# Three unread products ahead of each step's sum in the two gather passes of a graph network kernel

## Time and profile before

| | |
|---|---|
| median of three runs | 7530.44 us |
| the profiled execution: its own time | 7527.34 us |
| its span | 7525.2 us |
| TensorE (PE) busy | 6260.3 us, 83% of the span |
| TensorE weight loads (PEld) busy | 4862.5 us, 65% |
| VectorE (DVE) busy | 3390.7 us, 45% |
| ScalarE (ACT) busy | 1942.3 us, 26% |
| GpSimd (POOL) busy | 2203.3 us, 29% |
| mean granted clock of TensorE | 0.888 |

### The profile page before, as it was taken

How to read it: one execution, slowest core, us unless ns; L and a number is a source line. 1 busy time by engine, 2 the same in 40 slices (tenths; PEclk the granted TensorE clock), 3 DMA queues, 4 the chain that set the end, 5 groups by cost and what they waited for, 6 DMA issues and landing times.

```text
span 7525.2 us, 106468 instructions
## 1 busy us (share of the span) xinstructions
PE 6260.3 (83%) x27439; PEld 4862.5 (65%) x27440; DVE 3390.7 (45%) x9448; ACT 1942.3 (26%) x5163; POOL 2203.3 (29%) x2534
## 2 busy tenths in 40 slices
PE   5888899999999999677776676999999966767766
PEld 3443577778887787555555554777778755555555
DVE  8876666631111222555565564222233324444443
ACT  3899600000000111111111112232233322222222
POOL 2000100010001111566666631000111126666664
PEclk8987899999999999777778788999999978888787
DMA  4777877797788777433333328888877743333332
GB/s 156 255 257 271 294 265 264 262 330 275 275 303 313 253 260 253 123 83 83 85 83 83 83 59 302 303 291 322 320 242 250 242 153 101 100 100 100 99 100 74
DMA packets 599449, 1517.98 MB, mean 202 GB/s; under 512 B 72695, under 2 KB 241506, under 8 KB 599203
## 3 DMA queue, kind: packets, MB, share of 16 engines
q1 hardware_dynamic: 465395, 1121.48, 42.1%
q0 software_dynamic: 133824, 393.46, 17.1%
HBM read 1198.77 MB, written 316.80 MB: 201 GB/s over the span
## 4 chain that ended last, share of the span: by engine, by line
PE 58%; another core or an unknown queue 11%; DVE 9%; issue 8%; DMA 6%; ACT 4%; DVEq 2%; ACTq 1%; SPq 1%; POOL 0%; POOLq 0%
PE psum L1347 33%; PE psum L1194 4%; PE psum L1640 3%; PE psum L1543 3%; DMA slab<-adj 2%; PE psum L1612 2%; PE psum L1496 2%; DMA g_own<-own_dram 2%; DVE acc L2576 2%; PE psum L1531 2%; PE psum L1624 2%; ACT staged L1721 2%; DVE hot_j L2317 1%; PE psum L1189 1%
## 5 line engine op out<-in xcount | busy, mean ns | idle before, releaser
L1347 PE MATMUL psum<-X,slab 128*128 128x512 f32 x12495 | 3110.5, 402 | 77.6 <-DMA slab<-adj 42.3
L1347 PEld LDWEIGHTS psum<-X,slab 128*128 128x128 f32 x12495 | 2348.4, 191 | 609.6 <-DVE g_x L2385 89.6
L2576 DVE TENSOR_TENSOR acc<-acc,psum 128x264 f32 (+1 forms) x1660 | 703.0, 424 | 1035.1 <-PE psum L1640 290.7
L1015 POOL DMA_DIRECT2D table<-s_tab x147 | 80.2, 545 | 1911.2 <-DVE s_tab L2074 1911.2
L1496 PE MATMUL psum<-hot_j,hot_key 128*128 128x392 bf16 x1592 | 535.3, 407 | 114.8 <-ACT psum L1710 70.5
L1531 PE MATMUL psum<-node_tabs,onehot_t 128*128 x1660 | 271.9, 303 | 358.0 <-ACT onehot_t L1832 345.1
L1531 PEld LDWEIGHTS psum<-node_tabs,onehot_t 128*128 128x128 f32 x1660 | 270.5, 245 | 401.4 <-issue 395.0
L1105 POOL DMA_INDIRECT ring<-gat_table,idx_slot x420 | 416.0, 990 | 248.5 <-ACT idx_slot L1827 121.3
L1496 PEld LDWEIGHTS psum<-hot_j,hot_key 128*128 128x128 bf16 x1592 | 227.3, 146 | 404.5 <-issue 366.8
L1105 POOL DMA_INDIRECT ring<-rel_table,idx_slot x420 | 413.8, 985 | 253.6 <-ACT idx_slot L1827 138.7
L1721 ACT CAST staged<-psum 128x392 fp32r<-128x392 f32 x808 | 410.4, 508 | 113.8 <-PE psum L1496 91.7
(11 more groups left out here) (422 smaller groups left out, 8113.6 us busy)
## 6 DMA issues: line engine op xcount, KB each, us to landing
slab<-adj SPq DMA_DIRECT2D x383, 1344.0 KB, 6.7
slab<-adj SPq DMA_DIRECT2D x313, 896.0 KB, 6.0
adj<-staged SPq DMA_DIRECT2D x808, 196.0 KB, 1.9
X<-table SPq DMA_DIRECT2D x32, 1792.0 KB, 13.3
table<-s_tab POOLq DMA_DIRECT2D x196, 256.0 KB, 3.5
g_own<-own_dram POOLq DMA_DIRECT2D x35, 896.0 KB, 8.3
own_dram<-s_out POOLq DMA_DIRECT2D x196, 128.0 KB, 5.3
table<-tab_b SPq DMA_DIRECT2D x7, 1792.0 KB, 6.7
```

Of the source, the lines that this page charges most:

```text
L1347: last = nc.tensor.matmul(sums_of(j), slab[:, slab_at(c), u, j * P:(j + 1) * P], X[:, x_at(p, d), :], start=(d == 0), stop=(d == KT - 1))
L2576: V.tensor_tensor(a, a, psum[:, bank, 0:w], ALU.add).then_inc(sem("summed"), 1)
```

## The change

A helper `kept_busy(bank)` issues three products of 128 columns, of bf16 data that lies in SBUF at that time (the node numbers, `node_loc`), into columns 320 to 447 of the bank that the step's sum is to use. Nobody reads these columns. It is called ahead of each of the 830 sums in each of the two passes. The wait for `summed`, which says that the bank was read, moves ahead of the products, and the waits for the message (GAT) or for the gathered rows and the one-hot (FI) stay behind them. At the head of the GAT pass TensorE waits once for the copy of the transposed edges, which writes `node_loc`.

```diff
+        UNREAD = 320
...
+            IDLE_MM = 3
+
+            def kept_busy(bank):
+
+                for _ in range(IDLE_MM):
+                    nc.tensor.matmul(psum[:, bank, UNREAD:UNREAD + P], node_loc[:, 0:P], node_loc[:, 0:P], start=True, stop=True)
+
             def gat_half(n, r, tiles):
...
                 for v in range(HALF):
+                    pe.wait_ge(*ev("summed", n * HALF + (v + 1)))
+                    kept_busy(v)
                     pe.wait_ge(*ev("msg", n * HALF + (v + 1)))
-                    pe.wait_ge(*ev("summed", n * HALF + (v + 1)))
                     nc.tensor.matmul(psum[:, v, 0:GW], onehot[:, r * HALF + v, :], homes[r][:, v, :],
                                      start=True, stop=True).then_inc(sem("mm"), 1)
...
+            pe.wait_ge(*ev("edge_T_read", len(EDGE_BATCHES)))
             for n in range(2):
...
                         r, v = r0 + u // HALF, u % HALF
+                        pe.wait_ge(*ev("summed", i * U + (STEPS + u + 1)))
+                        kept_busy(u % GB)
                         if r < 2 or v == 0:
                             pe.wait_ge(*ev(home(FI, r, v), landed(i * 2 + u // HALF, r)))
                         pe.wait_ge(*ev("onehot", i * U + (ONEHOTS[FI] + u + 1)))
-                        pe.wait_ge(*ev("summed", i * U + (STEPS + u + 1)))
                         nc.tensor.matmul(psum[:, u % GB, 0:D], onehot[:, u, :], homes[r][:, v, 0:D],
                                          start=True, stop=True).then_inc(sem("mm"), 1)
```

## The result

The changed kernel takes 7622.06 us (median of 4 runs, 7615.52 to 7629.56), the one before 7529.53 us (4 runs, 7521.02 to 7533.01): a ratio of 1.0125 (95% interval 1.0107 to 1.0142), slower by 92 us where 12 were forecast. It lies in the range, and on the side that had the larger chance, but outside the forecast case's own range (7495 to 7590).

The account below looks back on a forecast made before the run. The prediction took the loop of GpSimd's gathers and TensorE's late reports of finished work as the bound. From 7527.3 us, +7 in GAT and +8 in FI gave 7542 us, range 7400 to 7690.

Parts of the forecast that it names:

- forecast case: The prediction's main case for the whole kernel, 7542 us, with its own range 7495 to 7590; chance 0.50.
- What bounds the kernel: GAT and FI passes: GpSimd and TensorE's reports form a loop, neither busy all of it; 270.1 and 247.9 us of waits.
- Price of a product: TensorE, both passes: 0.055 us at full clock, 0.108 at half; 382 us in all beside 816 us idle.
- GAT, second half: Second five steps of a GAT round: 0.17 us of products fits into 0.39 us idle, cost 0; uncovered 71 us.
- GAT, first half: First five steps of a GAT round: late row numbers +37 us, shorter late reports -30 us; value +7 us.
- FI, +8 us: Last edge pass: idle time covers the added products, cost 0, +8 taken for some rounds' ends; uncovered 130 us.
- The new wait and the swapped ones: Wait at GAT's head for copies some 2000 us earlier, and reordered waits before the sums: cost 0.
- The clock: Mean granted clock rises to 0.80 to 0.86 in GAT, 0.85 to 0.92 in FI; GAT's fall in the pause stays.
- Rival 1: Both passes: TensorE stays at full clock, reports come sooner; 130 to 260 us less, 7270 to 7400 us; chance 0.24.
- Rival 2: Both passes: late reports begin sooner, gathers go in fives; 7710 us, or 7620 for one half in eight; chance 0.20.
- Rival 3: The change doesn't do what it says: clock and times stay, 7530 us; chance 0.06.
- The signs named in advance: Right: remote idle near 600 us, GpSimd waits near 500; wrong: waits below 400 or runs of five the rule.

## Why the prediction was right in sign and wrong in size

**What bounds the kernel: right on the chips of the comparison.** The loop between GpSimd and TensorE's reports sets the pace, not TensorE's busy time. The last chip shows it: there the late reports are absent, and both passes fall to the gathers' own pace, 1130 / 830 = 1.36 and 1080 / 830 = 1.30 us each. The six-product kernel has the highest clock of its chip in both passes and is the slowest of the kernels with full products.

**Price of a product: right at its own spacing, short for a step.** The forecast had 0.055 and 0.108 us. Steps of one and six products give (1.63 - 1.09) / 5 = 0.11 us at the half clock, and at the full one (3700.99 - 3700.15 with six, 3702.78 - 3702.23 with one) (0.84 - 0.55) / 5 = 0.06. The Trainium skill's 56 and 107 ns (TensorE: Matmul & The Clock Gate, Part 1), for which before had no row, agree with both. But the first product of a step costs 0.21 at the half clock, so three take 0.43 us and not 0.32, and at the full clock 0.22 (0.67 - 0.45) and not 0.17.

**GAT, second half, cost 0: not contradicted.** At the full clock the steps keep ahead of what GpSimd waits for. No run isolates it.

**GAT, first half: +7 us, 41 measured.** The chain in it is right: exposed products, later sums, row numbers late. The +37 us were the delay of the sixth gather, once in a round, 0.5 us in 74 rounds. The -30 us were to come back, because a broken run has a shorter pause at its end. The credit is borne out as far as the pauses tell: at before's own prices, 40 more broken rounds (40 runs of ten fewer, 80 of five more) give 40 x (3.73 - 3.06) = 27 us back. It is the +37 that was too small. The pause behind a run of five grew from 1.68 to 2.16 us, 136 times, and behind a run of ten from 3.73 to 4.02, 12 times: 65 + 3 = 69 us. The delay came behind both halves of a broken round, not once in a round. 69 - 27 - 3 us of shorter gathers is 39 of the 41. This split is arithmetic on the pauses; which rounds break is not chance, and no run isolates the two terms.

**FI, +8 us: the term that failed most, 53 measured.** The cover was put at "about 1 us to spare" for the copy of row numbers, read from one round, and the products in front of it at 0.3 to 0.6 us: cost 0. The kernel with row numbers one sum late (0.9 us at the half clock) shows that there is less to spare in half of the rounds: it broke 40 of 80 runs of ten and cost 84 us. In the changed kernel 36 broke, for 1.0 us each, and the 44 whole ones have 0.5 us more behind them: 58 us, less 4 of shorter gathers. The forecast had no term for a run that breaks here. The upper bound of 130 us, the cover gone, was the better guide.

**The new wait and the swapped ones, 0: right**, 1.0003 (0.9992 to 1.0014) with no product.

**The clock: right** (0.81 and 0.87; forecast 0.80 to 0.86 and 0.85 to 0.92), and so was the reason that GAT's fall stays: the wait for the one-hots' copy lies ahead of the logits, where the change puts no product, and in after's round, too, the logits behind it run at the half clock (from 3724.68, ten passes in 2.31 us).

**Rivals.** Rival 1 (faster) failed on the chips of the comparison. It needed GpSimd's row numbers to come sooner; the late one-hot reports did shrink, but the waits that count grew. Rival 2 named the mechanism that decided in FI, row numbers for five gathers instead of ten; its sum for one half in eight, 7620, is what was measured. That the figure agrees is luck, for it had the rest wrong: 3 to 4 us were expected behind each five, and 2.2 were found, in far more than an eighth of the halves. It is a mild loss that is common, not a heavy one that is rare, and in GAT it is not the break that costs but the longer pause. Part of it came as rival 2 has it, with reports of the sums late (147.6 us against 42.7), part by plain exposure (208.5 against 121.3); the trace doesn't separate them further. Rival 3 (no effect) is out.

**The signs named in advance** went half against the forecast: L1831's remote waits fell from 608.6 to 360.3 us where they were to stay near 600, GpSimd's waits rose from 518 to 320.3 + 327.8 = 648 us where they were to stay near 500, and runs of five became the rule in GAT, which was written down as a sign of rival 2. The clock and the time outside the passes came as said.

**What the prediction did not see** is that its verdict may hang on the chip. Each sign was measured, on different chips, though not with one and the same kernel.

## What to carry to other kernels

Filler work that is meant to hold an engine's clock stands in front of the real work just when the clock is low and the work is late: price it at the half clock, with what it adds inside the work behind it, and look at who waits for the result there. Where a producer runs in bursts, ask in which places of a round a small delay can fall, and read the price of a cut burst from the pauses on both sides less the usual one: here it was dear in one pass and free in the other. And before tuning around a stall that the trace calls remote, look at the same code on another chip; the kernel before took over 400 of some 7500 us less where this one was absent.

## What the runs showed of the hardware

- TensorE's late reports: during an unbroken run of gathers, at the full clock, ScalarE gets reports of finished work up to 10.5 us late, about when the run has ended (608.6 us of "remote" waits in before's GAT pass). In after, eight places of that pass have three or more instructions in a row of TensorE that come one in 0.70 to 0.74 us although nothing in the profile holds them. Late reports are absent in the GAT pass that stayed at the half clock, present with runs of five at a clock of 0.90 (349.1 us, 3.6 us at most), and on one chip they don't occur at the full clock either. What causes them is open.
- Three products of one column a step leave TensorE at the half clock for a whole GAT pass, at 0.50 with 1582 of 1599 us busy, where three of 128 columns have 0.81 with 1091 of 1385. In the FI pass of the same kernel the clock is 0.84.
- A step of one fp32 sum of 264 columns takes 0.88 us at the half clock; with three bf16 products of one column ahead of it 1.32, with twelve 1.55; with one, three and six of 128 columns 1.09, 1.31 and 1.63; with three of 192 columns 1.41.
- The GAT pass of 830 steps with three one-column products, at the half clock throughout, took 1596 us, and with no product, at a mean clock of 0.76 and on another chip, 1312.
